# Attention with a mixture of experts: the mask's terms written into the score banks by ScalarE

## The reference, cut to what matters

```python
sim = einsum(q, k) * 8 + attn_bias            # q and k of length 1
sim = where(causal, -max, sim)
sim = where(mask, sim, -max)
x = x + layernorm(softmax(sim) @ v @ Wout)
x = x + moe(x)
```

## Time and profile before

| what | value |
|---|---|
| median of 3 runs | 1048.13 us (1047.93 to 1050.3) |
| the profiled execution | 1048.86 us, its span 1047.1 us |
| TensorE busy | 1006.9 us, 96% |
| VectorE busy | 703.5 us, 67% |
| ScalarE busy | 523.6 us, 50% |
| GpSimd busy | 437.4 us, 42% |
| granted TensorE clock, mean | 0.997 |

### The profile page before, as it was taken

One profiled execution on the slowest core, in us unless ns is written; L12 is line 12 of the kernel. 1 busy time (PEld: TensorE's weight loads), 2 busy tenths in 40 slices (PEclk: granted clock), 3 DMA queues, 4 the chain that ended last, 5 costly groups with the idle time before them and its releaser, 6 DMA issues.

```text
span 1047.1 us, 19955 instructions
## 1 busy us (share of the span) xinstructions
PE 1006.9 (96%) x6774; PEld 811.3 (77%) x6774; DVE 703.5 (67%) x2459; ACT 523.6 (50%) x1556; POOL 437.4 (42%) x422
## 2 busy tenths in 40 slices
PE   3878999999999999999999999999999999999998
PEld 2656977778777887778777797777877788777877
DVE  8887677765867558674777657676586755856553
ACT  3588256652566345662466615655256633565220
POOL 1645155443364344451545415454335434444212
PEclk9999999999999999999999999999999999999999
DMA  5220305121331112321132212321133111232042
GB/s 201 78 75 2 125 7 172 62 92 61 102 102 61 62 41 90 104 71 42 61 105 69 71 62 61 113 71 42 61 98 105 62 41 42 86 107 72 22 141 101
DMA packets 39539, 82.21 MB, mean 79 GB/s; under 512 B 4032, under 2 KB 18880, under 8 KB 39184
## 3 DMA queue, kind: packets, MB, share of 16 engines
q1 hardware_dynamic: 38480, 78.32, 22.8%
q10 hardware_dynamic: 960, 2.62, 0.7%
HBM read 71.33 MB, written 9.60 MB: 77 GB/s over the span
## 4 chain that ended last, share of the span: by engine, by line
PE 83%; DVE 8%; issue 2%; ACT 2%; DVEq 0%; POOL 0%
PE psY L1685 14%; PE psS L1552 7%; PE psG L70 6%; PE psG L72 6%; PE psG L71 6%; PE psO L1588 6%; PE psT L1563 5%; PE psS L1548 3%; PE psS L71 3%; PE psS L70 3%; PE psS L72 3%; PE psT L1570 2%; PE psO L1591 2%; PE psT L70 2%; PE psT L72 2%
## 5 line engine op out<-in xcount | busy, mean ns | idle before, releaser
L634 POOL TENSOR_TENSOR work<-work,rden 128x514 f32<-128x514 f32 x128 | 134.3, 1049 | 313.8 <-DVE rden L1179 313.8
L1685 PE MATMUL psY<-Wd,H 128*128 128x256 f32 x640 | 171.7, 397 | 0.0
L782 ACT ACTIVATE work<-work,low 128x257 f32<-128x257 f32 x256 | 128.3, 502 | 54.7 <-DVE low L1197 53.7
L70 PE MATMUL psG<-x1T_hi,Wgu 128*128 128x512 f32 (+1 forms) x292 | 134.7, 461 | 2.1 <-ACT leaky L826 1.9
L1685 PEld LDWEIGHTS psY<-Wd,H 128*128 128x128 f32 x640 | 111.7, 189 | 29.0 <-issue 14.6
L1197 DVE CUSTOM_DVE_ANT_0 work<-psS,bias,null_s 128x256 f32<-128x256 f32 x256 | 113.2, 479 | 24.3 <-PE psS L1552 22.8
L1293 DVE SCALAR_TENSOR_TENSOR leaky<-leaky 128x512 f32<-128x512 f32 x80 | 57.0, 713 | 103.2 <-ACT leaky L826 102.3
L623 POOL TENSOR_TENSOR rq<-qss,neghalf 128x16 f32<-128x16 f32 x32 | 97.6, 3050 | 43.8 <-DVE qss L1173 43.8
L72 PE MATMUL psG<-x1T_lo,Wgu 128*128 128x512 f32 (+1 forms) x292 | 114.5, 392 | 0.0
L71 PE MATMUL psG<-x1T_hi,Wgu 128*128 128x512 f32 (+1 forms) x292 | 114.0, 390 | 0.0
L1552 PE MATMUL psS<-KB,qT 64*128 64x256 f32 (+1 forms) x1024 | 105.8, 326 | 0.0
(11 more groups left out here) (262 smaller groups left out, 2288.9 us busy)
## 6 DMA issues: line engine op xcount, KB each, us to landing
Wgu<-wexp SPq DMA_DIRECT2D x70, 512.0 KB, 3.4
Wb<-wscr SPq DMA_DIRECT2D x64, 256.0 KB, 3.7
wexp<-Wgu SPq DMA_DIRECT2D x10, 512.0 KB, 3.3
xres<-in_x SPq DMA_DIRECT2D x8, 512.0 KB, 3.8
xin<-in_x SPq DMA_DIRECT2D x7, 512.0 KB, 4.5
out<-work SPq DMA_DIRECT2D x7, 512.0 KB, 3.0
raw<-in_wgu SPq DMA_DIRECT2D x10, 256.0 KB, 4.6
bias<-bscr SPq DMA_DIRECT2D x4, 512.0 KB, 5.9
```

The lines of the kernel that those rows point to most:

```text
L70: te.matmul(dst, a_hi, b_hi, start=start, stop=False)
L634: pool.tensor_tensor(T1[sl][:, hs, :], T1[sl][:, hs, :], rden[sl][:, 1, hs].unsqueeze(2) .to_broadcast([P, 2, N + 1]), ALU.mult)
L782: act.activation(T1[sl][:, h, :], T1[sl][:, h, :], ACT.Exp, scale=-1.0, bias=low[sl][:, 1, h:h + 1], accum_out=den[sl][:, 1, h:h + 1])
L1685: mm = te.matmul(psY[:, t // 2, (t % 2) * D:(t % 2 + 1) * D], H[:, k % H_RING, t * P:(t + 1) * P], Wd[:, ORDER[k], :], start=(k == 0 and t ...
```

## The change

From round 1 on, and there from step 1 on, the mask products are gone. ScalarE writes `MK` into both banks behind the four exponentials of the step before (`put_mask`), and the score products add to what is there (`start=False`). `score` waits for that write (`mask_ps`) in place of VectorE's reads; the write stands behind exponentials that have waited for both reads. Step 0 of each round, and the whole of round 0, keep the mask products. Since ScalarE needs the mask in every partition, `load_mask` now spreads it over 128 partitions, by two transfers.

```diff
--- before.py
+++ after.py
@@ -335,7 +335,7 @@
 
         xin_in = events("xin_in", 16)
         xres_in = events("xres_in", 16)
-        mask_in = events("mask_in", 64)
+        mask_in = events("mask_in", 32)
         wscr_in = events("wscr_in", 16, 16)
         wb_in = [events(f"wb_in{i}", 16 * (E // WB_RING)) for i in range(WB_RING)]
         out_in = events("out_in", 16, 16)
@@ -377,6 +377,7 @@
         qs_done = events("qs_done", TILES)
         qT_a = events("qT_a", TILES)
         exp_done = events("exp_done", GROUPS * STEPS)
+        mask_ps = events("mask_ps", ALL - 1)
         pt1_done = events("pt1_done", GROUPS * STEPS)
         x1T_a = events("x1T_a", KC)
         lex_done = events("lex_done", 1)
@@ -479,11 +480,10 @@
 
                 need(sp, mk_done, r - 1, 1)
                 stand(sp, waited_sp)
-                for i in range(2):
-                    for a, b in ((0, N), (N, P)):
-                        sp.dma_start(mask8[i * DH:i * DH + 1, :, a:a + b],
-                                     mask[:, bass.ds(r * TOK, TOK)].rearrange("a (b j) -> a b j", b=BB)[:, :, 0:b]) \
-                            .then_inc(mask_in.sem, 16)
+                for a, b in ((0, N), (N, P)):
+                    sp.dma_start(mask8[:, :, a:a + b],
+                                 mask[:, bass.ds(r * TOK, TOK)].rearrange("a (b j) -> a b j", b=BB)[:, :, 0:b]
+                                 .to_broadcast([P, BB, b])).then_inc(mask_in.sem, 16)
 
             def load_round(r):
                 load_mask(r)
@@ -756,7 +756,7 @@
                     if n >= VALUE_LAG:
                         head_out(r, n - VALUE_LAG)
                     if n < ALL:
-                        exps(r, n // STEPS, n % STEPS)
+                        exps(r, n // STEPS, n % STEPS, moe)
                     if moe is not None and n in GATE_AT:
                         take_gate(moe, GATE_AT[n])
                     if moe is None and 0 <= n - SPLIT_AT < W_RING:
@@ -774,7 +774,12 @@
                 act.activation(oT[0][:, STEPS * (g % 2) + s, (g // 2) * N:(g // 2 + 1) * N], value_bank(n)[:, 0:N],
                                ACT.Copy).then_inc(o_lead.sem, 1)
 
-            def exps(r, g, s):
+            def put_mask(r, n):
+
+                act.activation(psS[:, :, 0:N + P], MK[:, n // STEPS // 2, :].unsqueeze(1).to_broadcast([P, 2, N + P]),
+                               ACT.Copy).then_inc(mask_ps.sem, 1)
+
+            def exps(r, g, s, moe):
                 sl = g % 2
                 n = g * STEPS + s
                 need(act, s1_read, r, n + 1)
@@ -786,6 +791,8 @@
                     last = act.activation(T0[sl][:, h, :], T0[sl][:, h, :], ACT.Exp, scale=-1.0,
                                           bias=low[sl][:, 0, h:h + 1], accum_out=den[sl][:, 0, h:h + 1])
                 last.then_inc(exp_done.sem, 1)
+                if moe is not None and n + 1 < ALL:
+                    put_mask(r, n + 1)
 
             def turned(r, n):
                 need(act, pt1_ps, r, n + 1)
@@ -1032,7 +1039,7 @@
                     ins = dve.tensor_tensor(kd[:, :, i, :], kn[:], qk_scale[:].unsqueeze(1)
                                             .to_broadcast([P, TILES, DH]), ALU.mult)
                 ins.then_inc(kd_done.sem, 1)
-                need(dve, mask_in, r, 64)
+                need(dve, mask_in, r, 32)
                 dve.tensor_scalar(MK[:], mask8[:], -BIG, BIG, ALU.mult, ALU.add).then_inc(mk_done.sem, 1)
                 sum_q(r, 1)
                 if moe is not None:
@@ -1479,7 +1486,7 @@
                         need(te, qT_a, r, 2)
                         need(te, qT_v, r, 2)
                     if n < ALL:
-                        score(r, n // STEPS, n % STEPS)
+                        score(r, n // STEPS, n % STEPS, moe)
                     if n == VALUE_LAG and moe is not None:
 
                         need(te, wT_done, moe, 1)
@@ -1535,22 +1542,26 @@
                 if following is not None:
                     q_first(following)
 
-            def score(r, g, s):
+            def score(r, g, s, moe):
 
                 bb, p = g // 2, STEPS * (g % 2) + s
                 n = g * STEPS + s
                 q0 = bb * N
 
-                need(te, s1_read, r, n)
-                need(te, s0_read, r, n)
-                for i in range(2):
-                    half = slice(i * DH, (i + 1) * DH)
-                    te.matmul(psS[:, i, 0:N + P], pick_bf[half, :], MK[half, bb, :], start=True, stop=False)
+                added = moe is not None and n > 0
+                if not added:
+                    need(te, s1_read, r, n)
+                    need(te, s0_read, r, n)
+                    for i in range(2):
+                        half = slice(i * DH, (i + 1) * DH)
+                        te.matmul(psS[:, i, 0:N + P], pick_bf[half, :], MK[half, bb, :], start=True, stop=False)
+                else:
+                    need(te, mask_ps, moe, n)
                 for first, q1, keys_ in ((0, q0 + P, N), (N, q0, P)):
                     for i in range(2):
                         half = slice(i * DH, (i + 1) * DH)
                         mm = te.matmul(psS[:, i, first:first + keys_], qT[half, p, q1:q1 + P], KB[half, bb, 0:keys_],
-                                       start=False, stop=(first == N))
+                                       start=False, stop=(first == N or added), skip_group_check=added)
                 mm.then_inc(s_ps.sem, 1)
 
             def turn(r, n):
```

## The result

| | before | after |
|---|---|---|
| median | 1048.13 us (1047.93 to 1050.3) | 1106.84 us (1105.6 to 1107.67, 4 runs) |
| profiled execution, its span | 1048.86, 1047.1 us | 1106.85, 1105.1 us |
| granted TensorE clock, mean | 0.997 | 0.989 |

The ratio is 1.0554 (95% interval 1.0536 to 1.0573): slower by 5.5%, 58 us. The forecast was 1105 us.

What follows compares the result with a forecast made beforehand. The prediction took TensorE's matmuls to bound the kernel, and the change to close a 4.70 us loop through ScalarE's write. To 1048.9 us it added 50.6 for steps and 6 for the clock: 1105 us, range 1090 to 1125.

Steps and rivals of the forecast that it cites:

- The loop: Score products, VectorE's reads, exponentials, mask write and handover back to TensorE: no step shorter than 4.70 us.
- The write: ScalarE's new 128x768 mask write into PSUM: 0.81 us, midway between copies of 0.589 and 1.028.
- The rival with the cheaper write: ScalarE's PSUM write costs 0.59 us, the loop 4.48; 1079 us in all; chance 0.16.
- What it saves: Mask pairs removed from TensorE: 105 x 0.17 = 18 us, real only in steps TensorE sets; step 6 at 4.98.
- What it moves: Gate's copy starts at 4.56, leak at 5.19, so later reads come late; 7.6 us more a round, 50.6 together.
- the late ones: Steps 5, 10, 14 (step 9 alike), whose bank reads come 0.37 us late: 5.07 us each.
- The clock: TensorE's clock falls around step 12's wait of almost 3 us: 1.0 us in each of six rounds, 6 us.
- The sum: Whole program: 1048.9 + 50.6 + 6 = 1105.5, forecast as 1105 us.
- The edits at nothing: Wider mask load by 2 transfers, kept mask products in round 0 and step 0, and one wait for two: no cost.
- The clock that falls in short steps too: One more 1.2 GHz stretch a round at steps 0 and 1: 1117 us, some 1137 with a dear write; chance 0.15.
- The loop that does not bind (the other side): The write costs next to nothing, the loop is 4.0 us; total between 1042 and 1048; chance 0.05.

Runs made afterwards that it cites:

- e2_short: Changed kernel, with ScalarE's write covering only 64 of the 384 columns of each bank, the other mask terms left out; 1068.7 us, ratio 1.0203.
- e8_vector_some: Kernel before, with VectorE writing the mask for steps 3 to 8 and 10 to 15, and the normalization spread over steps 12, 14, 15, 16; 1038.59 us.
- e4_load_only: Kernel before, with the mask loaded into 128 partitions by two transfers and TensorE's mask products kept; 1048.91 us, ratio 1.0011.
- e3_spread: Changed kernel, with VectorE normalizing the next input tile by tile in steps 12, 14, 15, 16, not all in step 11; 1081.17 us, ratio 1.0321.
- e1_between: Changed kernel, with ScalarE's mask write moved between the first and second pair of exponentials; 1074.07 us, ratio 1.0258.
- e6_gate_first: Changed kernel, with the gate's copy ahead of the mask's write on ScalarE; 1118.41 us, ratio 1.0666.

## Why the prediction was right

**The loop.** Forecast 4.70; short steps measured 4.67 to 4.71. In step 6 the first read came 1.12 behind the products (forecast 1.02 + 0.11), the exponentials 0.93 later, the write from 3.82 to 4.61. In a step that ends with the wait the write ends at 4.62 and the products start at 4.67: a handover of 0.05, the 0.05 of the earlier trace rows. e2_short shows that the write ends the loop in these steps.

**The write.** Forecast 0.81, from midway between the two copies of the earlier trace rows; measured 0.792 in 105 rows that lie within 10 ns. The rival with the cheaper write falls. The Trainium skill, "ScalarE: Activation LUTs", Step-by-step, says that ScalarE writes to PSUM faster than to SBUF. This case's trace agrees at most weakly: 0.792 is 0.018 us or 2% below the midpoint of its copies into SBUF, which is 2 us over 105 writes, and those copies read PSUM, so that no two rows differ in the destination alone.

**What it saves.** Right in the step that it was worked out for: step 6 was forecast at 4.98 and measured 4.96 to 4.99. But the text sets 105 x 0.17 = 18 us as TensorE's own work beside it, and the runs show that a pair is not worth that, even where nobody waits: products that no longer follow a pair take 0.92 instead of 0.82, in e8_vector_some too, where nothing is waited for. Their weights used to load beside the pair, from 0.17 ahead of the products at 673.82 in the earlier trace rows. The weight loads (PEld) of that step before:

```profile
673.65 0.79 PEld L1552 LDWEIGHTS psS<-KB,qT 64*128 64x128 f32 x8
```

In e8_vector_some the products at 666.23 have theirs at 666.22, so nothing hides the first of them. A pair is worth 0.17 - 0.10 = 0.07, and the 0.06 to 0.065 measured for each write of e8_vector_some is close to it.

**What it moves.** The gate's copy was forecast at 4.56 and started at 4.55, the leak at 5.19 and 5.16. Steps 5, 9 and 10 came out at 5.04 or 5.05 for 5.07, step 7 at 5.07 for 5.12, step 12 at 7.41 for 7.53. Steps 11 and 13 without the fall of the clock take 4.75 for 4.70, since TensorE and not the loop sets them. Step 14 was listed with the late ones at 5.07 and took 4.98: behind the longer step 13 its reads came on time in four of the six rounds (1.12 behind its products) and 0.1 and 0.2 late in the others, and TensorE set the step. In round 7, without a fall of the clock, they came 0.3 late, the write ended just in time, and step 14 took 4.98 as well. So the 5.07 was wrong apart from the clock: step 13 takes 4.75 and not 4.70, and step 14's own work is 4.98. VectorE's rows of round 5, from step 11 into step 12, answer to the earlier trace rows:

```profile
742.33 0.69 DVE L1300 SCALAR_TENSOR_TENSOR leaky<-leaky 128x512 f32<-128x512 f32 x1 [2.27 <-ACT leaky L833]
...
743.02 2.38 DVE L891 TENSOR_SCALAR xin<-xin,mv,rstd 128x256 f32<-128x256 f32 x4
...
745.79 0.47 DVE L1204 CUSTOM_DVE_ANT_0 work<-psS,bias,null_s 128x256 f32<-128x256 f32 x1
```

From leak to reads it is 745.79 - 742.33 = 3.46, the 3.47 of before, and the reads come 3.88 after step 12's products at 741.91. The whole lateness goes into TensorE's wait.

**The clock.** Here a size was off. Stretches of round 5 of the changed kernel, steps 12, 13 and 14 (length, then busy us and count of PE, PEld, DVE, ACT, POOL, then the granted clock and DMA):

```profile
741.90:749.30 7.40, 4.84 (x33) 3.70 (x32) 6.22 (x21) 3.85 (x13) 2.73 (x3) 0.99 0.47 162
749.30:755.60 6.30, 6.28 (x34) 4.59 (x34) 1.86 (x9) 3.59 (x12) 1.85 (x3) 0.74 0.00 0
755.60:760.60 5.00, 5.00 (x37) 3.87 (x36) 3.55 (x14) 3.90 (x13) 1.62 (x2) 1.00 0.00 0
```

Step 13 is full of matmuls (6.28 of 6.30) at a granted clock of 0.74, a mixture of the 2.4 and 1.2 GHz levels. The fall came as forecast, once in each of the six rounds and behind step 12 (in round 6 it lasted twice as long). The term "1.0 in each of six rounds" was too low. Step 13 takes 6.34 instead of 4.75, so it is 1.6 in most rounds, and 10.9 in all instead of 6. The prediction let part of the cost fall into the loop's slack; step 13 has none, since TensorE sets it.

**The sum.** Forecast were 45.8 for the steps of six rounds, 6 for the clock and 4.8 for the last round. Measured are 54.2 - 10.9 = 43.3, 10.9 and 4.7. In rounds 2 to 6 the steps are 0.5 a round shorter than forecast, most of it in steps 0 to 4 and 8 (28.1 for 28.4), 12 and 14. Round 0, 2.0 shorter, and the stretches between rounds, at the start and at the end, 1.1 longer, were not forecast. The errors are of a few us each and partly cancel, so that 1105 lies within 2 us of 1106.84 is partly luck. The edits at nothing were nothing, as e4_load_only shows.

**The rivals.** The cheaper write falls by its rows. The clock that falls in short steps too falls by e3_spread, whose short steps kept their waits, while every fall behind round 0 was gone. The loop that does not bind (the other side) falls by 69 waits. e2_short shows how far it was: with a third of the write's length, the change still loses 2%.

## What to carry to other kernels

Before work is taken off the bound engine and given to one that looks idle (ScalarE was 50% busy), count the loop it closes, from the start of the bound engine's step through every instruction queued ahead of the moved work and back: here 4.70 us against steps of 3.4 to 5.1. Put the moved work at the earliest point where its data are free, on the engine that frees them (VectorE's reads freed the banks), and only in the steps where that engine has slack. Price the removed instruction by how much earlier the work behind it ends, not by how much earlier it starts: here 0.07 and not 0.17.

## What the hardware showed that was not expected

- **One longer wait in a round lowered the clock, frequent short ones did not.** In rounds 1 to 6 of the changed kernel, e1_between and e2_short TensorE's longest wait for the write is at the end of step 12, and a step full of matmuls follows. Behind a wait of 2.6 us (the changed kernel) that step ran partly at 1.2 GHz six times out of six; behind 1.8 us (e1_between) and 1.7 us (e2_short) in two rounds of six, though the waits of rounds 2 to 6 are alike to 0.01 us and e1_between's longest, 2.0 in round 1, was without a fall; behind 1.5 us (e6_gate_first) or less never. Waits of 1.0 to 1.3 us behind steps 0 and 1 of these rounds, as the changed kernel has them, did it in no kernel. The length of one wait does not decide alone: in round 0 a wait of 1.14 us behind step 12 was followed by a fall in the kernel before, and one of 1.13 in the same place of the changed kernel was not. What else decides stays open. The Trainium skill, "TensorE: Matmul & The Clock Gate", A second HAM failure mode, describes frequent tiny pauses between groups of matmuls that lower the clock again and again; the short steps of rounds 1 to 7, with pauses of 0.5 to 1.3 us one after another, do not show that.
- **Round 0's length differs from profile to profile.** Its 15 steps took from 45.0 us (e8_vector_some) to 49.4 (e1_between, e6_gate_first). Of that, 1.8 us is the normalization: the three kernels that spread it have 2.77 for step 12 of round 0 instead of 4.54. The rest goes with the stretches at the lower clock, which fall differently, and it need not belong to the kernel: executions of the kernel before took from 1046.98 us at a mean clock of 1.000 to 1050.67 at 0.993. That is as much as some of the differences above, and it is why e1_between's time says less than its steps do. What places these stretches was not tried and stays open.
- **Writing 128x768 into PSUM took ScalarE 792 ns and VectorE 961 ns.** From e2_short's 258 ns for 128x128, ScalarE's slope is (792 - 258) / 640 = 0.83 ns per column.
